# Cross-attention in a decoder: exponentials from key-by-token scores, heads from turned probabilities as stationary

## The chip, the cores and the metric

The kernel runs on one core of one Trainium2 chip. The metric is the device time of one launch in microseconds (us). The engines are TensorE (PE; its weight loads are PEld), VectorE (DVE), ScalarE (ACT), GpSimd (POOL) and SyncE (SP), which issues the DMAs. TensorE's clock is granted at 2.4 GHz (1.0 in the profile) or at half of it, 1.2 GHz (0.5).

## The reference

A decoder of four layers, each with self-attention, cross-attention and a feed-forward part, twelve sublayers, with `x = layernorm(x + sublayer(x))` after each. There are 32 sequences of 128 tokens and 128 features, all float32, and a context of 77 keys for each sequence. The change touches the cross-attentions of the layers 1, 2 and 3, which are of this kind (16 heads of 8 features):

```python
q = split_heads(xq @ Wq + bq); k = split_heads(xk @ Wk + bk); v = split_heads(xv @ Wv + bv)
logits = jnp.einsum('bhqd,bhkd->bhqk', q, k) / jnp.sqrt(8)
logits = logits + mask[None, None, :, :] * -1e9      # layer 2; layer 1 has no mask
weights = jax.nn.softmax(logits, axis=-1)
attn = jnp.einsum('bhqk,bhkd->bqhd', weights, v).reshape(B, S, 128)
return attn @ Wo + bo
```

Layer 3 has no biases, multiplies the scores by the square root of 8 and sets those where its mask (one row per sequence and token) is 0 to the lowest float32.

## The kernel before

A hardware loop makes four passes over eight sequences each. In a pass the twelve sublayers follow each other; their names in the code are L0A, L0X, L0F, L1A, L1X, L1F, L2A, L2X, L2F, L3A, L3X, L3F (A self-attention, X cross-attention, F feed-forward). The eight sequences are two groups `g` of four (`b`), a sequence is `j = 4 g + b`. Every engine runs its own program written out by hand, in order; semaphores (`wait_ge`, `then_inc`) tie them together. The weights of even layers share the buffer `w_even`, those of odd ones `w_odd`; SyncE loads a layer's weights once the layer two before is done. The rest lies in two arenas. PSUM has eight banks of 512 float32 columns.

The three cross-attentions L1X, L2X and L3X are built by one set of functions, `pe_context`, `act_context`, `dve_context` and `pool_context`; L3A, the self-attention of layer 3, uses some of the same helpers with 128 keys and keeps them in the change. Ahead of a stage `pe_context_part` and `act_context_part` make the keys and values of all eight sequences from the context: the keys in four copies (`C("res4")`), each with every fourth head's rows and zeros in the others, the values with zeros between (zeroed by GpSimd). So 32 rows of queries against one copy give four heads' scores with a contraction over 32 rows.

The unit of the loop is half a sequence, `u` of 16, which is 8 heads. In iteration `i` TensorE's program does

- `scores(i)` (L1402): two matmuls, 32 rows each, in the row groups 2 half + 0 and 1, tokens on the partitions, 4 x 77 columns each, into two of the four banks 0 to 3
- `pe_heads(i - 3)` (L1239): eight matmuls with 32 columns of values stationary and the turned probabilities moving
- `pe_probs_turn(i - 2)` (L1222): eight transposes of a head's 128x77 probabilities into banks 4 and 5.

Between them VectorE takes the maximum over the keys and subtracts it (L1290, L1292; with a mask, scale and mask first, L1283, then L1286 and L1288), ScalarE takes the exponential of 128x616 in SBUF (L1254), VectorE sums it and takes the reciprocal (L1299, L1301), GpSimd multiplies (L1314), and ScalarE and VectorE each copy one bank of turned probabilities out of PSUM (L1261, L1308). ScalarE adds the value bias to the heads of a group (L1267), and `pe_project_heads` (L1247) multiplies by Wo. The state is turned by `pe_turn_state` (L159) and multiplied by Wq (L1377). The second group's queries are made inside the loop, the first group's projection at `i == 12`; in L1X the first gate-up products of the next sublayer (L1539) lie between the last units.

A float32 matmul is two instructions in the profile, a transpose one.

## Time and profile before

| | |
|---|---|
| median of 3 runs | 5787.46 us |
| lowest and highest | 5780.36 and 5790.4 us |
| span of the profiled execution | 5793.5 us |
| instructions | 57753 |
| mean granted clock of TensorE | 0.836 |
| TensorE, VectorE, ScalarE, GpSimd busy | 85%, 51%, 33%, 18% |
| L1X, L2X, L3X in the first pass, first to last matmul | 107.7, 109.6, 110.5 us |

The profiled execution is one execution; its own time is the span, and it isn't among the three timed runs. Busy time is an average over twelve sublayers with different limits. The rows further down are the ones that bear on the three cross-attentions. Idle time stands in square brackets with what ended it. Where a line of the timeline has several instructions, the second number is the time from the first one's start to the last one's end, and the end of a matmul overlaps the start of the next.

### The profile page before, as it was taken

To read this page: it belongs to the slowest core of one execution; us is meant where nothing else is said; L and a number is where in the kernel's file an instruction comes from. 1 tells how busy PE (TensorE), PEld (TensorE's weight loads), DVE (VectorE), ACT (ScalarE), POOL (GpSimd) and SP (SyncE) were. 2 spreads that over 40 slices of the span, in tenths; PEclk is the share of its full clock that TensorE was granted. 3 is DMA by queue.
4 is the path that set the end of the run, shared out by engine and by line. 5 is a ranking of instruction groups with operands and counts; after the bars stand their busy time and mean duration, and the time that the engine had idled before them with its cause. 6 is when DMAs were issued, how large, how long until landed. Compare 5 with 4: busy or idle time off the path is not lost. (4 is left out here: it accounts for less than half of the span.)

```text
span 5793.5 us, 57753 instructions
## 1 busy us (share of the span) xinstructions
PE 4923.2 (85%) x20360; PEld 2783.9 (48%) x20360; DVE 2980.6 (51%) x6224; ACT 1939.1 (33%) x3508; POOL 1042.2 (18%) x876
## 2 busy tenths in 40 slices
PE   6888899989688889998968888998886888899888
PEld 4445454653444545465344454445534455545553
DVE  5555443763555544376355554446535555534643
ACT  4242222336324222233632422222364242223235
POOL 2021100213202110021320211002222021100222
PEclk8896879969799777996879987898597998789869
DMA  2000100000100010000010001000001000100000
GB/s 75 1 3 24 52 5 2 1 16 0 51 1 3 24 52 5 2 1 15 0 51 1 3 24 52 5 2 16 1 1 50 1 3 24 52 5 2 16 1 4
DMA packets 20876, 93.08 MB, mean 16 GB/s; under 512 B 5228, under 2 KB 14444, under 8 KB 17796
## 3 DMA queue, kind: packets, MB, share of 16 engines
q1 hardware_dynamic: 20580, 89.26, 4.1%
q8 instruction: 170, 2.79, 0.2%
q14 instruction: 126, 1.03, 0.1%
HBM read 87.16 MB, written 2.10 MB: 15 GB/s over the span
## 5 line engine op out<-in xcount | busy, mean ns | idle before, releaser
L1314 POOL TENSOR_TENSOR arena<-arena 128x616 f32<-128x616 f32 (+1 forms) x256 | 355.0, 1387 | 1189.2 <-DVE arena L1301 1188.8
L1254 ACT ACTIVATE arena<-arena 128x616 f32<-128x616 f32 (+1 forms) x256 | 205.2, 802 | 930.7 <-DVE arena L1288 481.2
L1222 PE MATMUL ps<-const,arena 128*77 128x128 f32 (+1 forms) x2048 | 422.0, 373 | 69.1 <-POOL arena L1314 69.1
L210 POOL TENSOR_SCALAR rstd_e<-mean_var 128x4 f32<-128x4 f32 x120 | 27.4, 228 | 2467.8 <-DVE mean_var L176 2467.8
L1923 DVE TENSOR_TENSOR arena<-ps,arena 128x512 f32<-128x512 f32 x256 | 176.5, 691 | 468.7 <-ACT arena L1873 468.7
L1222 PEld LDWEIGHTS ps<-const,arena 128*77 128x77 f32 (+1 forms) x2048 | 340.1, 207 | 153.6 <-POOL arena L1314 82.2
L1239 PE MATMUL ps<-arena,w_even 77*32 77x128 f32 (+1 forms) x2560 | 352.9, 355 | 50.8 <-DVE arena L1308 50.4
L1873 ACT ACTIVATE arena<-ps 128x512 f32<-128x512 f32 x288 | 172.0, 597 | 607.9 <-PE ps L1821 607.9
L1239 PEld LDWEIGHTS ps<-arena,w_even 77*32 77x32 f32 (+1 forms) x2560 | 264.3, 141 | 190.8 <-ACT arena L1261 87.1
L2263 PE MATMUL ps<-w_even,w_odd 128*128 128x512 f32 x640 | 321.6, 649 | 26.9 <-issue 26.9
L1308 DVE COPY arena<-ps 77x512 f32<-77x512 f32 (+1 forms) x256 | 174.5, 682 | 270.2 <-PE ps L1222 270.1
L1820 PE MATMUL ps<-xT,w_even 128*128 128x512 f32 x576 | 308.9, 618 | 3.1 <-DVE arena L1910 3.1
L1827 PE MATMUL ps<-arena,w_even 128*128 128x512 f32 x576 | 295.0, 594 | 7.0 <-DVE arena L1923 4.7
L745 PE MATMUL ps<-xT,w_even 128*128 128x512 f32 (+1 forms) x544 | 269.2, 618 | 0.4
L1821 PE MATMUL ps<-arena,w_even 128*128 128x512 f32 x512 | 266.3, 602 | 0.0
L1261 ACT ACTIVATE arena<-ps 77x512 f32<-77x512 f32 (+1 forms) x256 | 151.0, 590 | 328.7 <-PE ps L1222 328.5
L1402 PE MATMUL ps<-arena 32*128 32x308 f32 x768 | 211.3, 663 | 41.8 <-DVE arena L1288 25.2
L199 DVE TENSOR_TENSOR y_tok<-ps,x_tok 128x512 f32<-128x512 f32 x72 | 49.4, 686 | 357.3 <-PE ps L683 265.5
L1299 DVE TENSOR_REDUCE arena<-arena 128x8 f32<-128x616 f32 (+1 forms) x256 | 228.2, 892 | 0.5
L1559 PE MATMUL ps<-arena,w_odd 128*128 128x512 f32 x512 | 220.4, 592 | 0.0
L2263 PEld LDWEIGHTS ps<-w_even,w_odd 128*128 128x128 f32 x640 | 125.2, 205 | 186.9 <-issue 179.2
L2467 DVE SCALAR_TENSOR_TENSOR arena<-ps,arena 128x512 f32<-128x512 f32 x48 | 33.2, 692 | 343.8 <-ACT arena L2352 342.9
(383 smaller groups left out, 9365.4 us busy)
## 6 DMA issues: line engine op xcount, KB each, us to landing
w_even<-in_w SPq DMA_DIRECT2D x4, 6916.0 KB, 19.2
w_even<-in_w SPq DMA_DIRECT2D x4, 3313.5 KB, 10.9
w_odd<-in_w SPq DMA_DIRECT2D x4, 2824.5 KB, 9.4
w_odd<-in_w SPq DMA_DIRECT2D x4, 2095.0 KB, 8.2
w_odd<-in_w SPq DMA_DIRECT2D x4, 2048.0 KB, 15.2
x_in<-in_x SPq DMA_DIRECT2D x10, 256.0 KB, 2.8
w_odd<-in_w SPq DMA_DIRECT2D x4, 577.0 KB, 3.6
w<-in_w SPq DMA_DIRECT2D x1, 2050.0 KB, 10.7
```

Of the source, the lines that this page charges most:

```text
L745: mm = nc.tensor.matmul(ps[0:rows, k + i % 2, :], lhsT, xT[g][:, :], start=True, stop=True)
L1222: mm = nc.tensor.transpose(ps[0:nk, 4 + h // 4, (h % 4) * P:(h % 4 + 1) * P], m["P"][u % 3][:, h, :], ident)
L1239: mm = nc.tensor.matmul(ps[c0:c0 + 32, 6 + g, b * P:(b + 1) * P], m["v"][g][0:nk, b, r, c0:c0 + 32], m["PT"][0:nk, 4 * i + r, :], start=(r ...
L1254: nc.scalar.activation(p, p, ACT.Exp, scale=scale).then_inc(c_exp.sem, 1)
L1299: nc.vector.tensor_reduce(m["sum"][u % 3], m["P"][u % 3], AX.X, ALU.add)
L1314: nc.gpsimd.tensor_tensor(m["P"][u % 3], m["P"][u % 3], bcast(m["sum"][u % 3], m["nk"]), ALU.mult)\
L1402: mm = nc.tensor.matmul(ps[:, 2 * (u % 2) + i, 0:4 * KC], m["q"][g][r:r + 32, b * P:(b + 1) * P], m["k"][g][r:r + 32, b, :, :], start=True ...
L1559: mm = nc.tensor.matmul(bank(4 + n % 2), W(L1F, w)[:, k * T + c * P:k * T + (c + 1) * P], src[g][:, k, :], start=(k == 0), stop=(k == 3))
L1820: nc.tensor.matmul(bank(i % 2), w1, xT[g][:, :], start=True, stop=True)
L1821: nc.tensor.matmul(bank(2 + i % 2), w3, x3, start=True, stop=True).then_inc(e_gu.sem, 1)
L1827: nc.tensor.matmul(bank(6 + g), w, e_h[i % 2], start=(n == 0), stop=(n == 35)).then_inc(e_down.sem, 1)
L2263: nc.tensor.matmul(o, W(L3F, "ew2")[:, p * 384 + m * P:p * 384 + (m + 1) * P], i_hm[g][4 * (j - 1) + p], start=(p == 0), stop=False)
```

## The change

The scores are computed twice, once with the tokens on the partitions for the maximum alone, and once with the keys on the partitions for the exponential. A unit is a whole sequence, `j` of 8.

- `scores(j, p)`: the same two matmuls as before, for two values of `p`, now always into banks 0 and 1. `maxima` takes the negated maximum of them straight from PSUM. In L3X the mask is added in PSUM, by a bf16 matmul of the identity with the mask; in L2X VectorE adds it.
- `split_max` writes the 16 maxima as three bf16 parts, `turn_max` turns them with one bf16 transpose, and `by_head` spreads them (multiplied by the constant 0/1 columns `mrow`) into `less`, a moving operand of 512 columns.
- `turned_scores(j)`: four float32 matmuls, keys as stationary (32 rows x 77 columns) and queries in four copies as moving (512 columns), one in each row group, into banks 2 to 5. L2X first puts the mask into these banks with 16 transposes, L3X adds it with four bf16 matmuls. `less_max` adds the negated maximum with four bf16 matmuls.
- ScalarE reads these banks with the exponential and writes the turned probabilities to SBUF (four of 77x512 for a sequence). VectorE's subtraction, sums and copies, ScalarE's copies, GpSimd's multiplication and the 16 transposes of a sequence go.
- `heads(j)`: 16 matmuls with a head's turned probabilities (77x128) as stationary and its values with a column of ones (77x9) moving. `scaled` divides by the ninth column on VectorE, `turn_heads` turns the result, ScalarE copies it with the value bias.
- The queries are copied four times by ScalarE (`act_context_queries`), the keys once more. The end of the stage has another order. `w_loaded` uses two semaphores in place of ten.

```diff
+        def act_context_queries(act, L, g):
+            m = CB[L]
+            act.wait_ge(c_qc.sem, c_qc[L, g])
+            for r in range(4):
+                kw = {} if L == L3X else {"bias": m["bq"][:, r:r + 1]}
+                i = nc.scalar.activation(m["qx"][g][:, :, r, :], bank(6 + g).rearrange("p (b t) -> p b t", b=NB),
+                                         ACT.Identity, scale=m["rs"][:, r:r + 1], **kw)
+            i.then_inc(k_qx.sem, 1)
...
+                def scores(j, p):
...
+                    if j or p:
+                        pe.wait_ge(k_mr.sem, k_mr[L, j, p] - 1)
                     for i in range(2):
-                        r = 32 * (2 * half + i)
-                        mm = nc.tensor.matmul(ps[:, 2 * (u % 2) + i, 0:4 * KC], m["q"][g][r:r + 32, b * P:(b + 1) * P],
-                                              m["k"][g][r:r + 32, b, :, :], start=True, stop=True,
-                                              tile_position=(r, 0))
-                    mm.then_inc(c_sc.sem, 1)
+                        r = 32 * (2 * p + i)
+                        mm = nc.tensor.matmul(ps[:, i, 0:4 * KC], m["q"][g][r:r + 32, b * P:(b + 1) * P],
+                                              m["kx"][g][r:r + 32, b, :, :], start=True, stop=(L != L3X),
+                                              tile_position=(r, 0), skip_group_check=True)
+                    if L == L3X:
+                        for i in range(2):
+                            mm = nc.tensor.matmul(ps[:, i, 0:4 * KC], ident_bf[:, :], m["neg"][:, j, :]
+                                                  .rearrange("p (r k) -> p r k", r=1).to_broadcast([P, 4, KC]),
+                                                  start=False, stop=True, skip_group_check=True)
+                    mm.then_inc(k_s.sem, 1)
+
+                def turned_scores(j):
...
+                    for c in range(4):
+                        if j:
+                            pe.wait_ge(k_ex.sem, k_ex[L, j - 1, c])
+                        o = bank(2 + c)[0:KC, :]
+                        if L == L2X:
+                            for r in range(4):
+                                nc.tensor.matmul(o[:, r * P:(r + 1) * P], m["neg"], ident, is_transpose=True,
+                                                 start=(r == 0), stop=False, skip_group_check=True)
+                    for c in range(4):
+                        r = 32 * c
+                        nc.tensor.matmul(bank(2 + c)[0:KC, :], m["k"][g][r:r + 32, b * KC:(b + 1) * KC],
+                                         m["qx"][g][r:r + 32, b, :, :], start=(L != L2X), stop=False,
+                                         tile_position=(r, 0), skip_group_check=True)
+                    if L == L3X:
+                        for c in range(4):
+                            nc.tensor.matmul(bank(2 + c)[0:KC, :], ident_bf[0:KC, 0:KC],
+                                             m["negT"][:, j * P:(j + 1) * P].rearrange("p (r t) -> p r t", r=1)
+                                             .to_broadcast([KC, 4, P]), start=False, stop=False, skip_group_check=True)
+
+                def less_max(j):
+                    pe.wait_ge(k_mx.sem, k_mx[L, j])
+                    for c in range(4):
+                        r = 32 * c
+                        nc.tensor.matmul(bank(2 + c)[0:KC, :], ones_bf[r:r + 32, 0:KC], m["less"][j % 2][r:r + 32, :],
+                                         start=False, stop=True, tile_position=(r, 0), skip_group_check=True)\
+                            .then_inc(k_st.sem, 1)
...
+                def heads(j):
+                    if j:
+                        pe.wait_ge(k_oc.sem, k_oc[L, j - 1])
+                    for h in range(16):
+                        c, r = divmod(h, 4)
+                        if r == 0:
+                            pe.wait_ge(k_ex.sem, k_ex[L, j, c])
+                        mm = nc.tensor.matmul(heads_psum(j)[:, h, :], m["PT"][j % 2][:, c, r * P:(r + 1) * P],
+                                              m["v"][:, j, h, :], start=True, stop=True)
+                    mm.then_inc(k_pv.sem, 1)
...
+                for i in range(8 + 3):
+                    if i < 8:
+                        scores(i, 0)
                     if 0 <= i - 3:
-                        pe_heads(pe, L, i - 3)
-                    if 0 <= i - 2 < 16:
-                        pe_probs_turn(pe, L, i - 2)
-                    if i == 12:
+                        turn_heads(i - 3)
+                    if 0 <= i - 1 < 8:
+                        turn_max(i - 1)
+                        turned_scores(i - 1)
+                    if i == 1:
+                        pe_turn_state(pe, PREV[L], 1)
+                    if i < 8:
+                        scores(i, 1)
+                    if i == 2:
+                        pe.wait_ge(xT_ready.sem, xT_ready[PREV[L], 1])
+                        nc.tensor.matmul(bank(7), W(L, "Wq"), xT[1][:, :], start=True, stop=True)\
+                            .then_inc(c_qp.sem, 1)
+                    if 0 <= i - 1 < 8:
+                        less_max(i - 1)
+                    if 0 <= i - 2 < 8:
+                        heads(i - 2)
+                    if i == 7:
                         pe_project_heads(pe, L, 0)
```

ScalarE's loop is, for `i` from 1 to 10, `heads(i - 3)` (the copy), the state's copy at 1, `act_context_queries` at 2, `exps(i - 1)`. VectorE's is `maxima(i, 0)`, `by_head(i - 1)`, `maxima(i, 1)`, `split_max(i)`, the norm of the state at 0, the second group's queries at 2, `scaled(i - 2)`, and the first group's sum at 8 and norm at 9. GpSimd does the bias sums and the norms' powers alone.

## Rows read from the trace of the kernel before

**Rows 1.** The page: busy time, share of the span, instructions.
```profile
PE 4923.2 (85%) x20360; PEld 2783.9 (48%) x20360; DVE 2980.6 (51%) x6224; ACT 1939.1 (33%) x3508; POOL 1042.2 (18%) x876
```

**Rows 2.** Windows: L1X in three passes, L2X twice, L3X, middle of L1X.
```profile
core 0: us, PE busy (x) PEld busy (x) DVE busy (x) ACT busy (x) POOL busy (x), PEclk, DMA share, GB/s
449.81:557.50 107.69, 93.86 (x482) 65.23 (x482) 57.78 (x109) 24.47 (x38) 24.46 (x22) 0.62 0.07 28
1903.82:2003.49 99.67, 85.58 (x482) 59.78 (x482) 57.76 (x109) 24.46 (x38) 24.46 (x22) 0.67 0.08 30
3354.45:3444.22 89.77, 74.44 (x482) 52.97 (x482) 57.29 (x109) 24.35 (x38) 24.47 (x22) 0.77 0.09 33
...
675.62:785.18 109.56, 92.95 (x482) 66.43 (x482) 70.44 (x148) 23.21 (x37) 23.24 (x21) 0.58 0.12 50
...
1158.38:1268.85 110.47, 93.43 (x470) 65.38 (x470) 70.20 (x139) 22.51 (x36) 22.00 (x20) 0.58 0.06 20
461.00:523.00 62.00, 61.31 (x283) 41.36 (x283) 32.54 (x51) 14.28 (x22) 13.35 (x12) 0.50 0.00 1
```

**Rows 3.** Timeline of TensorE in L1X (start, us, group): low clock, then full.
```profile
482.42 1.40 PE L1402 MATMUL ps<-arena 32*128 32x308 f32 x4
483.74 2.78 PE L1239 MATMUL ps<-arena,w_even 77*32 77x128 f32 x16
486.45 1.99 PE L1222 MATMUL ps<-const,arena 128*77 128x128 f32 x8
488.37 1.40 PE L1402 MATMUL ps<-arena 32*128 32x308 f32 x4
...
528.32 1.10 PE L1222 MATMUL ps<-const,arena 128*77 128x128 f32 x8
529.35 0.79 PE L1402 MATMUL ps<-arena 32*128 32x308 f32 x4
```

**Rows 4.** Timeline: matmuls that move 8 columns, at low and at full clock.
```profile
1277.41 3.58 PE L2294 MATMUL ps<-w_odd,arena 32*128 32x8 f32 x16
...
817.92 1.06 PE L1786 MATMUL ps<-w_even,xT 128*128 128x8 f32 x8 [0.69 <-ACT xT L167]
```

**Rows 5.** Timeline of TensorE in L3A: one matmul of 32 rows, both clocks.
```profile
1059.61 2.07 PE L1999 MATMUL ps<-w_even 32*128 32x512 f32 x2
...
1072.11 1.12 PE L1999 MATMUL ps<-w_even 32*128 32x512 f32 x2
```

**Rows 6.** Timeline of TensorE in L3F: two bf16 matmuls at low clock.
```profile
1312.28 1.09 PE L2241 MATMUL ps<-arena,expand 8*128 8x512 bf16 x2 [0.26 <-ACT arena L2327]
```

**Rows 7.** Groups by line and form, L1X, first pass: busy us, mean ns.
```profile
L1290 DVE TENSOR_REDUCE arena<-ps 128x8 f32<-128x616 f32 x16 | 12.6, 790 | 11.6 <-PE ps L1402 11.6
L1261 ACT ACTIVATE arena<-ps 77x512 f32<-77x512 f32 x16 | 9.5, 593 | 33.1 <-PE ps L1222 33.1
L1267 ACT ACTIVATE arena<-ps,w_even 128x512 f32<-128x512 f32 x2 | 1.4, 680 | 3.6 <-PE ps L1239 3.6
```

**Rows 8.** Timeline of VectorE in L3F: a split into three bf16 parts.
```profile
1285.62 0.18 DVE L669 CAST arena<-arena 128x32 bf16<-128x32 f32 x1
...
1286.66 0.18 DVE L677 CAST arena<-arena 128x32 bf16<-128x32 f32 x1
```

**Rows 9.** One line's instructions: duration in ns, least, median, most.
```profile
L1343 ACT ACTIVATE arena<-ps,arena,const x64: 600/626/654, 437.8 to 4990.6; 128x308 f32<-128x308 f32 x64
```

**Rows 10.** Timeline of ScalarE ahead of L1X: the values' copies.
```profile
448.00 0.78 ACT L300 ACTIVATE w_even<-ps 77x128 f32<-77x128 f32 x4 [1.11 <-PE ps L1330]
```

**Rows 11.** Timeline of TensorE at the end of L1X, around a rise.
```profile
544.63 1.99 PE L1222 MATMUL ps<-const,arena 128*77 128x128 f32 x8
546.42 0.90 PE L159 MATMUL ps<-const,x_tok 128*128 128x128 f32 x4
```

**Rows 12.** Windows after a rise and before a fall, columns as in rows 2.
```profile
714.30:721.00 6.70, 5.58 (x50) 4.10 (x50) 6.22 (x12) 1.79 (x3) 2.58 (x3) 1.00 0.01 2
...
533.40:536.60 3.20, 0.22 (x3) 0.04 (x2) 3.13 (x9) 1.20 (x2) 0.99 (x2) 1.00 0.00 0
```

More of the change, by code:

```diff
@@ L1088, in act_l1a @@
             result(1)
+            act_context_queries(act, L1X, 0)
             act_context_part(act, L1X, "v")
@@ L1147, in build @@
         SMALL = [L1X, L2X, L3A, L3X]
+        CROSS = [L1X, L2X, L3X]
         U = range(16)
-        us = [(L, u) for L in SMALL for u in U]
+        us = [(L3A, u) for u in U]
         lg = [(L, g) for L in SMALL for g in G]
@@ new lines, in self_buffers @@
+            e = Carve(0, w_even, cols[L3X]["_width"])
+            o = Carve(0)
+            m["S"] = [e.take(NB * 16 * P).rearrange("p (m t) -> p m t", t=P),
+                      a.take(NB * 16 * P).rearrange("p (m t) -> p m t", t=P)]
+            m["v"] = [t.take(NB * 4 * P).rearrange("p (b r d) -> p b r d", b=NB, r=4) for t in (e, a)]
+            m["k"] = [t.take(NB * 4 * P).rearrange("p (b r k) -> p b r k", b=NB, r=4) for t in (e, w)]
+            m["q2"] = e.take(NG * T)
+            m["q"] = m["oT"] = [m["q2"][:, g * T:(g + 1) * T] for g in G]
@@ L1201, in buffers @@
+            m["Q"] = [o.take(16 * P).rearrange("p (t b h) -> p t b h", b=NG * NB, h=16) for _ in range(2)]
+            m["bk"] = a.take(4)
+            m["rs"] = a.take(4)
+            o = Carve(0, start=4352)
+            m["P"] = [o.take(8 * P).rearrange("p (m k) -> p m k", m=8) for _ in range(3)]
             m["PT"] = a.take(8 * P).rearrange("p (m q) -> p m q", m=8)
@@ L1351, in dve_context_columns @@
+        SCALE = {L1X: 1.0, L2X: float(np.float32(8.0) ** np.float32(-0.5)),
+                 L3X: float(np.float32(8.0) ** np.float32(0.5))}
         def dve_context_columns(dve, L):
             m = CB[L]
-            dve.wait_ge(w_loaded[L].sem, 16)
+            dve.wait_ge(*w_loaded(L))
+            nc.vector.tensor_scalar(m["rs"], C("res4"), SCALE[L], None, ALU.mult)
             if L != L3X:
                 nc.vector.tensor_scalar(m["bk"], C("res4"), W(L, "bk"), None, ALU.mult)
+                nc.vector.drain()
+                nc.vector.tensor_scalar(m["bq"], m["rs"], W(L, "bq"), None, ALU.mult)
@@ L1426, in run @@
                 if L == L1X:
+                    pe_turn_state(pe, L1X, 0)
+                    pe_l1f_gate_up(pe, 0)
                     pe_l1f_gate_up(pe, 1)
+                if L == L2X:
+                    pe_l2f_route(pe, 0)
                 pe_project_heads(pe, L, 1)
@@ L1456, in run @@
                 if L == L2X:
+                    act_copy_state(act, L2X, 0, xT[0][:, :])
                     act_l2f_exps(act, 0)
@@ L1483, in run @@
+                    if 0 <= i - 2:
+                        scaled(i - 2)
+                    if i == 8:
+                        dve_sum(dve, L, 0)
+                    if i == 8 and L == L1X:
+                        dve_l1f_scales(dve)
+                    if i == 9:
+                        dve_normalise(dve, L, 0, x_tok[0])
                 if L == L2X:
```

338 lines of the change are left out of this document (213 added, 125 removed).

## The prediction

> **What bounds the kernel now.** I read the page first. TensorE is busy 85% of the span, VectorE 51%, ScalarE 33%, GpSimd 18% [rows 1], but these are averages over twelve layers, and the change touches three stages. So next the stretches from the first to the last matmul of each. L1X takes 107.7, 99.7 and 89.8 us in the first three passes, the fourth like the third (mean 96.7), L2X 109.6 in the first and 113.1 in the others (mean 112.3), L3X 110.5 in all four [rows 2]. L1X is the same work every time; what differs is the granted clock, 0.62 to 0.77. In its middle (461 to 523 us) TensorE is busy 61.3 of 62 us at a clock of 0.50, while VectorE has 32.5 us to do. Hence the timeline of TensorE, where a half sequence (8 heads) is three steps: scores 1.32 us (482.42 to 483.74), heads 2.71, eight transposes 1.92, together 5.95, then the next begins. At full clock the transposes take 1.03, and the pair of score matmuls 0.79 in its own row [rows 3]. TensorE sets these stages wherever its clock is 1.2 GHz. So what GpSimd, VectorE and ScalarE are relieved of counts little; what counts is what TensorE is given to do for a sequence, against 11.9 us now, and at which clock.
>
> **The change, on TensorE, per sequence (16 heads), at 1.2 GHz.**
>
> Removed: 16 transposes (3.84) and the old heads (5.42). The four key-by-key score matmuls (two pairs, 2.64) stay, for the maximum alone.
>
> Heads with the probabilities as stationary: 16 float32 matmuls that move nine columns. They are bound by loading 128 columns: the row nearest in kind is L2294, 32x128 stationary and 8 moving columns, 16 instructions in 3.58 us, 0.22 each; the 128-row L1786 at full clock has 1.06 for eight, of which I count 0.92 (the next line begins then), 0.115 each [rows 4]. A float32 matmul is two instructions in these rows, so 32 x 0.22 = 7.0 us (3.7 at 2.4 GHz). 32 and 128 rows cost alike, so 77 will. This is more than the old heads.
>
> Turned scores: four matmuls of 32 rows x 512 columns, one in each row group. One alone is 2.07 at 1.2 GHz and 1.12 at 2.4 in its row, some 2.0 and 1.05 from its start to the next line's [rows 5]. Two in two row groups overlap: each moving 308 columns, they take 1.32, and 308/512 of 2.0 is 1.2. I take full overlap of four, 2.0; above, overlap only in pairs, 4.0. The Trainium skill, "TensorE: Matmul & The Clock Gate", section "Part 3: Packing small matmuls — row/col tiling", gives 3.07 for four row tiles of 512 columns instead of 4. By it the step is 8.0/3.07 = 2.6 us, and the sum would be 0.6 x 96 = 58 us more.
>
> The split maximum taken off: four bf16 matmuls of 512 columns, also by row group. Two in sequence take 1.09 [rows 6], about 0.5 each; overlapped 0.5, in pairs 1.0, in sequence 2.0. I take 0.5. Two single transposes (maximum in bf16, heads) at 0.15 to 0.25: 0.4.
>
> Sum for L1X: 2.6 + 2.0 + 0.5 + 7.0 + 0.4 = 12.5, against 11.9. L2X adds 16 transposes that put the mask into the turned scores, 16 x 0.24 = 3.8: 16.3. L3X adds four bf16 matmuls of 512 columns and four of 308: 1.8 + 1.1 = 2.9: 15.4. At 2.4 GHz the three are 6.7, 8.8 and 8.3.
>
> **The other engines.** VectorE: four reductions of 308 columns (616 take 0.79) 1.6, five small casts and subtractions (1285.62 to 1286.84) 1.2, one multiplication of 512 columns from PSUM 0.7 at the same rate, reciprocal and scaling at most as much: 4.2 us; L2X adds four additions of 308, near 6 [rows 7, 8]. ScalarE: four exponentials of 77x512 at 0.6 and a small copy, 2.7. GpSimd has nothing left but bias and norm. All are below TensorE, even at 2.4 GHz. Within an iteration the 3.7 to 7 us of heads stand between the maximum's matmuls and the next turned scores, which hides the exponentials; the turned scores hide the maxima, whose banks 0 and 1 are now single. So I cost these waits at nothing; without that cover ScalarE's 2.4 us would stand open.
>
> **Around the loop.** Before the values ScalarE now issues four copies of the queries (4 x 0.68) and two more of the keys (2 x 0.63); the values take two copies of 0.6 for twice 0.78 [rows 7, 9, 10]; queued behind them are the values for which the first scores wait: 2.2 us later in L1X and L3X (I let the keys' part overlap), 0.3 in L2X. The rest of L1X: queries 2.1, two turns of the state 1.9, two projections 3.1, the first two gate-up products 6.3 and some 6 us of waits at both ends: 19.4. At the end x_tok is normalised only after the last heads are scaled, so turn, copy and gate-up, which lay between units before, stand in a row. L2X: 14. L3X: 9. The old stages have 14 to 17 us in which TensorE is not busy [rows 2]; I have not carried them over but counted the new ends step by step. The weight transfers wait for the same stage ends as before; one semaphore for several layers costs nothing.
>
> All at 1.2 GHz: L1X 8 x 12.5 + 19.4 = 119.4; L2X 8 x 16.3 + 14 = 144.4; L3X 8 x 15.4 + 9 = 132.2.
>
> **The clock.** It is the largest unknown. In L1X it stayed at 1.2 GHz for ten units with no idle time. It rose near 547, right after eight transposes and amid four more, all of full height, and after another rise it was 1.00 for 6.7 us. It fell at the end of 3.2 us in which TensorE was busy 0.22 [rows 11, 12]. The nine-column matmuls stayed at 1.2 when they began there [rows 4]. For L1X and L3X I therefore take 1.2 GHz, with one short rise at the projection of the first four sequences: 2 us back in L1X; in L3X, where mask matmuls of full height stand beside the turned scores, 5 us. In L2X every sequence has 3.8 us of full-height transposes and 2.0 of turned scores: I let the clock rise in each, and fall in the heads. A stretch of 5 to 6 us at 2.4, somewhat less than that 6.7, does the work of 10 to 12: 5 us back a sequence, 40 in the stage.
>
> L1X 119.4 + 2.2 - 2 = 119.6 against 96.7: +22.9. L2X 144.4 + 0.3 - 40 = 104.7 against 112.3: -7.6. L3X 132.2 + 2.2 - 5 = 129.4 against 110.5: +18.9. Sum +34.2 a pass, times 4: +137 us. The profiled execution gives 5793.5 + 137 = 5930; its span is 0.1% above the median of the timed runs (5787.5), so I forecast 5787.5 + 137 = 5924.
>
> **Rivals.** *Transposes do not lift the clock.* Then L2X stays at 1.2 GHz, +32 instead of -8, and the sum is (23 + 32 + 19) x 4 = +297: 6085. Against it, the rise among transposes [rows 11]; for it, the long low stretch that is one third transposes [rows 3]. The Trainium skill, same page, section "Part 4: PE-mode transpose", says that they do not count as busy for the clock. By that rule this rival is the forecast; the trace speaks against it [rows 11, 12].
>
> *The clock is up for most of the three stages (the other side).* Four row groups work at once in the turned scores, more of the array than any old step of these stages used, and L1X itself ran at 0.77 in two passes [rows 2]. With 5 us back in every sequence of every stage: L1X 81.6 (-15), L2X 105 (-8), L3X 94 (-16), times 4: -156, 5632. It decides from 34 us more a pass than I give, about 2 us more for each sequence of L1X and L3X. At 2.4 GHz throughout, the stages would be some 70, 88 and 82 us: -320, 5470. Against it: more than half of a sequence's time is heads that stream nine columns.
>
> *The row groups overlap only in pairs.* 2.0 + 0.5 us more for each of 96 sequences: +240 on top, 6160. For it: no row shows four at once.
>
> *No effect.* GpSimd's and VectorE's waits at the stages' ends go away and the clock gives a little more, so that gain and loss cancel: 5787.
>
> **How the numbers follow.** Forecast with L1X and L3X low and L2X lifted in part: 0.52, its own range 5840 to 6000, from 3 to 7 us back in L2X and from none to 2 back in L3X. Transposes that don't lift: 0.14. Clock mostly up: 0.20. Pairs: 0.08. Cancelled: 0.06. A change within 0.2%, 12 us, is about what a measurement of this kernel can't tell from none. Slower 0.52 + 0.14 + 0.08 = 0.74, same 0.06, faster 0.20. The range 5760 to 6090 takes in the forecast, the cancelled case, the first rival and the edge of the second, and leaves out the deeper gains and the pairs.
>
> **What would show it.** Nine-column matmuls at 0.22 us an instruction (0.115 at full clock), 32 a sequence: if they are near 0.11 at 1.2 GHz, the largest term is wrong. Four turned-score matmuls starting within some ns of each other and over in 2.0 us. In L1X a period of 12.5 us a sequence at clock 0.50 with TensorE without idle time; in L2X one of about 11 with the clock between 0.6 and 0.8, up in the turned scores and down in the heads. ScalarE's and VectorE's releases must not end TensorE's waits inside the loop. A clock over 0.7 in L1X or L3X would make the forecast wrong, so would a TensorE that waits for exponentials or maxima.

## The result, and the profile after

The changed kernel takes 5838.3 us (median of 6 runs, 5827.2 to 5843.6), the kernel before took 5788.6 us beside it (6 runs, 5777.2 to 5794.3). The ratio is 1.0067, with a 95% interval from 1.0036 to 1.0097: slower, by about 50 us. The forecast was 5924 us, 137 us slower: the direction was right, the size was nearly three times too large. The profiled execution has a span of 5825.5 us, 32 us above that of before: it is the shortest of the six, 11 us under their median, and the profiled one of before is 5 us above its own. Every table by stage here comes from one profiled execution of a kernel.

First the page, its row for busy time, then windows of the stages (first matmul of the scores to last of the projection): L1X in the first two passes, L2X in the first two, L3X in the first and the third. The answers before are [rows 1, 2].

```profile
PE 5044.5 (87%) x20968; PEld 2864.4 (49%) x20968; DVE 2680.8 (46%) x6309; ACT 1972.4 (34%) x3632; POOL 781.9 (13%) x708
```

```profile
core 0: us, PE busy (x) PEld busy (x) DVE busy (x) ACT busy (x) POOL busy (x), PEclk, DMA share, GB/s
449.57:556.93 107.36, 101.60 (x466) 69.55 (x466) 35.81 (x120) 24.50 (x48) 5.05 (x6) 0.57 0.06 25
1902.91:2007.28 104.37, 98.45 (x466) 66.72 (x466) 36.09 (x122) 24.50 (x48) 5.04 (x6) 0.59 0.06 26
...
671.82:772.03 100.21, 91.90 (x594) 72.94 (x594) 50.11 (x155) 26.03 (x51) 3.81 (x5) 0.77 0.15 63
2120.78:2225.58 104.80, 96.26 (x594) 75.90 (x594) 50.10 (x155) 26.04 (x51) 3.81 (x5) 0.73 0.14 60
...
1148.26:1266.47 118.21, 112.09 (x518) 71.17 (x518) 35.14 (x114) 22.36 (x47) 2.51 (x4) 0.60 0.04 16
...
4056.37:4168.82 112.45, 106.33 (x518) 67.30 (x518) 35.14 (x114) 22.36 (x47) 2.51 (x4) 0.64 0.04 18
```

VectorE's and GpSimd's work is down (in L1X 57.8 to 36.1 us, 24.5 to 5.0), TensorE's is up, and TensorE is busy 92 to 95% of these stages. The three stages in a table (us, sums over four passes; "between" is everything else of the span):

| | before | after | difference | forecast |
|---|---|---|---|---|
| L1X | 386.9 | 418.8 | +31.9 | +91.6 |
| L2X | 449.0 | 414.6 | -34.4 | -30.4 |
| L3X | 441.9 | 467.1 | +25.2 | +75.6 |
| between | 4515.7 | 4525.0 | +9.3 | 0 |

So L2X came out as forecast, and two thirds of what L1X and L3X were to lose did not appear. Now the timeline of TensorE: a sequence of L1X with the clock at 0.50 and later heads of the same stage, one of L2X, one of L3X (start in us, us of the group, lines; instructions are x).

```profile
476.33 7.00 PE L1522 MATMUL ps<-w_even,arena 77*128 77x9 f32 x32
483.26 1.40 PE L1466 MATMUL ps<-arena 32*128 32x308 f32 x4
484.59 0.47 PE L1528 MATMUL ps<-const,arena 128*128 128x128 f32 x1
484.85 0.31 PE L1513 MATMUL ps<-ident_bf,arena 128*128 128x128 bf16 x1
485.10 2.00 PE L1490 MATMUL ps<-w_even,arena 32*77 32x512 f32 x8
486.88 0.64 PE L1503 MATMUL ps<-arena,ones_bf 32*77 32x512 bf16 x2
486.89 1.24 PE L1466 MATMUL ps<-arena 32*128 32x308 f32 x4
487.92 0.64 PE L1503 MATMUL ps<-arena,ones_bf 32*77 32x512 bf16 x2
488.49 7.00 PE L1522 MATMUL ps<-w_even,arena 77*128 77x9 f32 x32
...
500.61 3.99 PE L1522 MATMUL ps<-w_even,arena 77*128 77x9 f32 x32
...
719.55 3.32 PE L1486 MATMUL ps<-const,arena 128*77 128x128 f32 x16
722.80 1.10 PE L1490 MATMUL ps<-w_odd,arena 32*77 32x512 f32 x8
...
724.56 3.74 PE L1522 MATMUL ps<-arena 77*128 77x9 f32 x32
...
1174.04 2.00 PE L1490 MATMUL ps<-w_even,arena 32*77 32x512 f32 x8 [1.14 <-ACT arena L1580]
1175.98 1.93 PE L1495 MATMUL ps<-w_even,ident_bf 77*77 77x512 bf16 x4
...
1180.37 7.00 PE L1522 MATMUL ps<-w_even,arena 77*128 77x9 f32 x32
```

L1522 are the heads, L1466 the scores, L1490 the turned scores, L1486 and L1495 the mask, L1503 the maximum taken off. In L1X the period is 488.49 - 476.33 = 12.16 us, without an idle gap; 12.5 was forecast. The nine-column instructions take 7.00 / 32 = 0.22 us. Four turned-score matmuls are over in 2.00 us. The second pair of scores (486.89) runs in the row groups that the maximum's matmuls leave free. In L3X the next heads begin at 1195.90, 15.53 us after 1180.37 (forecast 15.4). The waits inside the loop, which the forecast put at nothing, are small: in the first pass 2.2 us for the split maxima in L2X's first two sequences and 1.1 us for exponentials in L3X (the row at 1174.04). The costs at the lower level of the clock were right; what was not is how long the clock stayed there.

### The profile page after: what moved, and what is told of

It reads as the page before. It is cut to its first block and busy times, and to the rows that moved or that the text cites. A ratio compares the mean times of both kernels' runs of the same rounds, so it can differ in the third digit from the quotient of the medians.

```text
span 5825.5 us, 58910 instructions
## 1 busy us (share of the span) xinstructions
PE 5044.5 (87%) x20968; PEld 2864.4 (49%) x20968; DVE 2680.8 (46%) x6309; ACT 1972.4 (34%) x3632; POOL 781.9 (13%) x708
## 5 line engine op out<-in xcount | busy, mean ns | idle before, releaser
L1522 PEld LDWEIGHTS ps<-w_even,arena 77*128 77x128 f32 x2048 | 367.1, 281 | 34.5 <-issue 27.0
L1522 PE MATMUL ps<-w_even,arena 77*128 77x9 f32 x2048 | 373.1, 325 | 3.3 <-ACT arena L1589 3.3
L1580 ACT ACTIVATE arena<-ps 77x512 f32<-77x512 f32 x384 | 196.1, 591 | 184.4 <-PE ps L1503 184.4
L1466 PE MATMUL ps<-arena 32*128 32x308 f32 x768 | 206.2, 624 | 47.0 <-DVE arena L1632 20.5
L823 ACT ACTIVATE arena<-ps,w_even 128x512 f32<-128x512 f32 (+1 forms) x136 | 93.4, 687 | 332.3 <-PE ps L752 332.3
L1632 DVE TENSOR_REDUCE arena<-ps 128x4 f32<-128x308 f32 x256 | 110.5, 473 | 206.2 <-PE ps L1471 137.8
L1666 DVE RECIPROCAL arena<-ps 128x16 f32<-128x16 f32 x96 | 24.7, 257 | 378.5 <-PE ps L1522 378.5
L2033 PEld LDWEIGHTS ps<-arena,w_even 128*128 128x128 f32 x576 | 108.8, 190 | 148.3 <-issue 133.8
L1330 POOL TENSOR_TENSOR arena<-arena 128x1024 f32<-128x1024 f32 x64 | 121.3, 1896 | 407.7 <-DVE arena L1317 407.3
L2740 POOL TENSOR_TENSOR w_even<-w_even,arena 128x512 f32<-128x512 f32 x128 | 143.9, 1151 | 221.7 <-ACT arena L2534 130.0
```

The source lines that it names most:

```text
L1466: mm = nc.tensor.matmul(ps[:, i, 0:4 * KC], m["q"][g][r:r + 32, b * P:(b + 1) * P], m["kx"][g][r:r + 32, b, :, :], start=True, stop=(L != ...
L1522: mm = nc.tensor.matmul(heads_psum(j)[:, h, :], m["PT"][j % 2][:, c, r * P:(r + 1) * P], m["v"][:, j, h, :], start=True, stop=True)
L1580: nc.scalar.activation(m["PT"][j % 2][:, c, :], bank(2 + c)[0:KC, :], ACT.Exp, scale=scale)\
L2033: nc.tensor.matmul(bank(6 + g), w, e_h[i % 2], start=(n == 0), stop=(n == 35)).then_inc(e_down.sem, 1)
L2740: nc.gpsimd.tensor_tensor(i_hm[g][4 * k + p], i_h[g][p], i_mb[g][4 * k + p], ALU.mult)\
```

## The experiments

All are built from the changed kernel unless they say otherwise. The ratio in each is to the kernel before, run beside it; the changed kernel has 1.0067. The kernel before itself came out between 5752 and 5837 us in these comparisons, with medians from 5777.7 to 5799.8, so the ratio counts more than the time. Three dots in an edit stand for lines left out.

**Mask transposes of L2X left out.**

```diff
-                        if L == L2X:
-                            for r in range(4):
-                                nc.tensor.matmul(o[:, r * P:(r + 1) * P], m["neg"], ident, is_transpose=True,
-                                                 start=(r == 0), stop=False, skip_group_check=True)
...
-                nc.vector.tensor_scalar(m["neg"], W(L, "mask"), -1000000000.0, None, ALU.mult)
+                nc.vector.tensor_scalar(m["neg"], W(L, "mask"), 0.0, None, ALU.mult)
```

> The changed kernel without the 16 transposes that put L2X's mask into its turned scores (the mask of L2X is left out altogether, its column of negated values is zero; all other work stays). Theory: full-height transposes raise the clock for the turned scores and heads behind them and so pay for themselves. Without them a sequence of L2X is one of L1X: the stage comes to L1X's 104.4 us less its own extras, 104.4 - 19.4 + 14 = 99 us, against 104.8 with them: -6 us a pass, 5815 us in all, and the granted clock of L2X falls from 0.73 to about 0.6. Rival: the transposes are a plain cost and the clock rises as often without them: the 3 us that they take in each sequence go, -24 us a pass, 5740 us.

Measured: 5837.0 us, 1.0071 (1.0049 to 1.0094), as with them. Window of L2X in the second pass:

```profile
2124.94:2231.34 106.40, 98.75 (x466) 68.93 (x466) 50.13 (x155) 26.07 (x51) 3.81 (x5) 0.55 0.14 59
```

128 instructions fewer (466 for 594), and the stage takes 106.4 us instead of 104.8: the clock is 0.55 in place of 0.73. Over the four passes L2X takes 425.5 us without them and 414.6 with them. The 16 transposes of a sequence cost nothing, because the clock rises after them. "Transposes do not lift the clock" falls.

**The same transposes, of zeros, added to L1X.** The result stays the reference's.

```diff
-                        if L == L2X:
+                        if L in (L1X, L2X):     # m["neg"] is zero in L1X
...
-                                         m["qx"][g][r:r + 32, b, :, :], start=(L != L2X), stop=False,
+                                         m["qx"][g][r:r + 32, b, :, :], start=(L == L3X), stop=False,
```

> The changed kernel with 16 float32 transposes of zeros added to each sequence of L1X, into the banks of the turned scores, where L2X has its mask transposes; the result is the same. Theory: they lift the clock, and L1X takes L2X's period of 10.0 us a sequence in place of 12.15 in those that are at 1.2 GHz and 9.15 in those that rose: 8 x 10.0 + 19.4 = 99 against 104.4: -5 us a pass, 5818 us, clock of L1X from 0.59 to 0.7 or more. Rival: they are only added work, 16 x 0.24 us at 1.2 GHz or 16 x 0.12 at 2.4: +15 to +31 us a pass, 5900 to 5960 us.

Measured: 5831.5 us, 1.0057 (1.0037 to 1.0077). L1X in the second pass:

```profile
1896.73:2001.37 104.64, 97.87 (x594) 75.24 (x594) 36.08 (x122) 24.50 (x48) 5.04 (x6) 0.76 0.06 25
```

104.6 us for 104.4 with 128 instructions more, and the clock at 0.76 for 0.59. The 5 us of gain expected are not there, the 15 to 31 us of the rival neither: work that lifts the clock paid for itself once more (417.8 us over four passes, for 418.8).

**Short full-height matmuls among the heads of L1X and L3X.**

```diff
                                               m["v"][:, j, h, :], start=True, stop=True)
+                        if L != L2X:
+                            for _ in range(2):
+                                mm = nc.tensor.matmul(ps[:, 6 + j // NB, 384:512], ident_bf[:, :], ident_bf[:, :],
+                                                      start=True, stop=True, skip_group_check=True)
```

> The changed kernel with two bf16 matmuls of the identity by itself (128 rows, 128 columns, into a free part of the heads' bank, never read) after each of the 16 heads in L1X and L3X. Theory: what keeps these stages at 1.2 GHz is that the nine-column matmuls of the heads keep little of the array at work; with full-height work among them the clock stays at 2.4 GHz, where heads take 3.7 and the added 32 matmuls at most 32 x 0.055 = 1.8 us. A sequence of L1X is then 6.7 + 1.8 = 8.5 us against 12.15, of L3X 10.1 against 15.5; L1X about 83 us (-20 or so), L3X about 95 (-23): -170 us in all, 5660 us. Rival: the clock of these stages does not depend on it; then the added matmuls cost 32 x 0.11 = 3.5 us a sequence at 1.2 GHz, +28 us a stage, +224 us: 6060 us.

Measured: 5961.1 us, 1.0284 (1.0244 to 1.0325). L1X and L3X in the second pass:

```profile
1942.51:2058.66 116.15, 110.28 (x722) 79.11 (x722) 36.08 (x122) 24.54 (x48) 5.05 (x6) 0.62 0.06 23
2655.53:2787.80 132.27, 127.29 (x774) 83.94 (x774) 35.16 (x114) 22.39 (x47) 2.52 (x4) 0.61 0.04 15
```

The clock stayed near where it was (0.62 and 0.61; in L1X 0.58 in two of the passes), and the 256 added instructions cost 15 us a pass in L1X and 16 in L3X (477.4 - 418.8 and 531.2 - 467.1, by four), a little over half of the rival's 28. My expectation was wrong: full-height work in this amount and form, spread through the heads, does not hold the clock, while a block of 16 transposes raises it. The two differ in type (bf16 and float32), in kind (matmul and transpose) and in place (spread and in one block); which of these matters is not shown, since no block of plain matmuls was tried.

**The change in L2X alone, and in L1X and L3X alone.** Both programs hold the old functions and the new ones, and a list says which stage has which.

```diff
-        CROSS = [L1X, L2X, L3X]
+        CROSS = [L2X]               # the other kernel: [L1X, L3X]
```

> The change made in L2X alone; L1X and L3X are built as before. Theory: the stages are independent and the whole is the sum of stage effects: L2X gains 449.0 - 414.6 = 34.4 us a launch, L1X and L3X go back to their old 386.9 and 441.9 us: 5787 - 34 = about 5755 us, 0.5 to 0.7% faster than before. Rival: what is gained in L2X is given back at its ends (the stretch behind L2X grew by 3.5 us a pass): no more than 0.3% faster, 5770 us or more.

> The change made in L1X and L3X alone; L2X as before. Theory A: stage effects add up and each stage has its own time whatever is around it: L1X 418.8 and L3X 467.1 us as in the changed kernel, L2X back at 449.0: 5838 + 34 = 5872 us. Theory B, after the L2X-only kernel, in which the unchanged L1X ran in 338 us at a clock of 0.83 in place of 387 at 0.71: the clock that a stage gets depends on when it starts, and the same stage comes out differently when the work around it shifts; then L1X is 5 us or more a pass away from 104.7, or L2X from 112.3, in either direction.

Measured: new L2X alone 5711.3 us, 0.9856 (0.9816 to 0.9895). New L1X and L3X with the old L2X: 5817.0 us, 1.0063 (1.0030 to 1.0095). Windows of the first: L1X (old) in the first two passes; then of the second: L2X (old) in the first two.

```profile
447.92:530.79 82.87, 67.55 (x482) 48.61 (x482) 57.41 (x109) 24.35 (x38) 24.48 (x22) 0.86 0.09 36
1874.64:1959.81 85.17, 70.23 (x482) 50.57 (x482) 57.37 (x109) 24.35 (x38) 24.48 (x22) 0.82 0.09 35
```

```profile
675.00:771.84 96.84, 74.74 (x482) 55.16 (x482) 69.28 (x148) 22.42 (x37) 23.22 (x21) 0.74 0.13 57
2120.70:2229.35 108.65, 96.55 (x482) 67.41 (x482) 70.75 (x148) 23.42 (x37) 23.21 (x21) 0.56 0.12 51
```

Of the first kernel's 82 us (span 5711.8), L2X gave 449.0 - 419.4 = 30 us, as expected. But 48 us came from the L1X that nobody had touched: 338.4 us instead of 386.9, with the same 482 matmul instructions and the clock at 0.82 to 0.86 instead of 0.62 to 0.77 [rows 2]. In the other kernel the old L2X took 96.8 us in two passes and 108.7 and 109.9 in the others, against 113.1 in three passes of before. Stage effects do not simply add up: an old stage gets another clock when the work around it changes. Of theory B the size came true in L2X (9 us a pass away from 112.3), not in L1X (1.7 us away from 104.7); its reason, the moment of the start, is not shown.

What sets the old L1X's times apart is when the clock rises. Windows of the kernel before, first pass, then third pass ahead of the rise and after it; then of new L2X alone, first pass, ahead of the rise and after it.

```profile
455.00:526.00 71.00, 66.29 (x304) 45.81 (x306) 38.12 (x61) 16.31 (x25) 15.82 (x13) 0.50 0.04 16
...
3360.00:3386.50 26.50, 22.14 (x96) 14.95 (x97) 14.11 (x23) 5.96 (x9) 6.08 (x5) 0.50 0.09 38
3387.00:3421.00 34.00, 30.87 (x265) 23.06 (x264) 30.65 (x58) 12.58 (x20) 12.22 (x11) 1.00 0.01 1
```

```profile
452.00:472.00 20.00, 15.06 (x70) 10.63 (x68) 13.08 (x23) 4.72 (x8) 5.24 (x5) 0.50 0.19 80
472.50:512.50 40.00, 35.21 (x295) 25.91 (x296) 35.01 (x65) 13.48 (x22) 14.19 (x13) 1.00 0.00 1
```

In the kernel before the rise inside the loop comes 77, 56 and 32 us after the stage's first matmul in the first three passes, with new L2X alone after 24 us, and from then on the clock stays up until TensorE waits 3 us for VectorE near the end of the loop. The earlier the rise, the shorter the stage: 107.7, 99.7, 89.8 and 82.9 us. What decides the moment is open.

**The same L1X begun a little later**, in the kernel before.

```diff
+                    if u == 0 and L == L1X:
+                        for _ in range(4):
+                            nc.tensor.matmul(ps[:, 2, 384:393], ident, ident[:, 0:9], start=True, stop=True)
```

> The kernel before with four more float32 matmuls of nine columns (never read) ahead of L1X's first scores, 0.9 us at 2.4 GHz or 1.8 at 1.2, in each pass, nothing else. Theory: the same L1X gets another clock when it starts at another moment; the added work is 4 to 7 us in all, but L1X comes out 5 us or more a pass away from its 107.7, 99.7, 89.8 and 89.8 us, up or down, so that the total is off by more than what was added. Rival: the differences between passes and kernels come from something else (data, the neighbouring stages), and all of L1X, L2X and L3X stay as they were but for the added 1 to 2 us: 5793 us.

Measured: 5783.2 us (12 runs, 5752.8 to 5842.3), 0.9996 (0.9963 to 1.0030). Inconclusive: the median did not move, and the runs of both kernels spread over 76 to 90 us (before: 5752.5 to 5828.8). The profiled execution took 5842.3 us, the longest of the twelve, so its stages are not compared. That the moment of the start decides is not shown.

**All turned-score matmuls of L1X in one row group**, those for the maximum too; three quarters of L1X's scores are computed from other heads' rows.

```diff
-                        r = 32 * c
+                        r = 0 if L == L1X else 32 * c      # in turned_scores and less_max
```

> The changed kernel with the four turned-score matmuls and the four that take off the maximum of L1X all in row group 0 instead of one in each (same shapes and count; the other groups' heads are left out of L1X's scores, so the result of L1X is another). Theory: the four groups run at once; in one group the turned scores take 4 x 2.0 = 8.0 us in place of 2.0 and the maximum's 4 x 0.5 = 2.0 in place of 0.5, part of it beside the scores of groups 2 and 3: +6 to +7.5 us a sequence, +48 to +60 us a pass if the clock stays, and the clock of L1X falls from 0.59 to 0.50, since fewer rows work at once, for another 5 to 10 us: +53 to +70 a pass, 6050 to 6120 us. Rival: the groups hardly overlap and the 2.0 us of the profile is something else (queued issue): less than +15 us a pass, below 5900 us.

Measured: 6051.4 us, 1.0452 (1.0377 to 1.0526). L1X in the second pass, the inside of its loop in the first pass, and a piece of its timeline:

```profile
1951.49:2110.98 159.49, 153.50 (x466) 89.91 (x466) 36.17 (x122) 24.44 (x48) 5.04 (x6) 0.52 0.04 17
...
450.00:600.00 150.00, 146.36 (x441) 86.79 (x440) 30.91 (x101) 23.41 (x47) 2.54 (x3) 0.50 0.00 1
```

```profile
1988.20 4.55 PE L1490 MATMUL ps<-w_even,arena 32*77 32x512 f32 x5
1991.69 1.40 PE L1466 MATMUL ps<-arena 32*128 32x308 f32 x4
1992.54 2.76 PE L1490 MATMUL ps<-w_even,arena 32*77 32x512 f32 x3
1995.10 1.91 PE L1503 MATMUL ps<-arena,ones_bf 32*77 32x512 bf16 x4
```

159.5 us instead of 104.4, +55 a pass, inside the expected 53 to 70. The eight instructions take from 1988.20 to 1995.10, 6.9 us instead of 1.8 (485.10 to 486.88): the four row groups do work at once, 3.9 times as fast as one. "Only in pairs" falls. The clock, too, shows something: in none of the four passes does it rise inside L1X's loop (0.50 from 450 to 600 us), where in the changed kernel it rises three or four times a pass. So what lifts the clock there in the changed kernel is the work of the row groups together; the turned scores and the maximum's matmuls were moved at once, so which of the two counts is not separated.

**ScalarE's copies of the first queries behind the values.**

```diff
-            act_context_queries(act, L1X, 0)
             act_context_part(act, L1X, "v")
+            act_context_queries(act, L1X, 0)       # and the same for L3X
```

> The changed kernel with ScalarE's four copies of the first group's queries issued behind the copies of the values in L1X and L3X, not ahead of them. Forecast's step: the copies ahead of the values make the first scores of L1X and L3X 2.2 us late. Theory after the trace of the changed kernel: only 1.5 us of it is there, in L3X alone, so L3X starts 1.5 us earlier a pass, L1X not, and the turned scores, which need these copies, take back part: 0 to -1.5 us a pass, 5832 to 5838 us, no difference that can be measured. Rival: the first term was right, only hidden by something else: -4 us a pass, 5820 us.

Measured: 5837.2 us, 1.0090 (1.0060 to 1.0120), no difference from the changed kernel. The stretches ahead of L1X and L3X got 2.0 and 5.4 us shorter over four passes, L1X and L3X 3.5 and 2.6 us longer: the copies can stand before or behind, the turned scores need them either way.

**Heads by column group in L1X and L3X.** The values are stationary again, and four matmuls in a row go to four different column groups; a second set with ones gives the sums.

```diff
+    for o, st in ((0, m["v"][g][0:KC, b]), (16 * 9, None)):
+        for r in range(4):
+            for c in range(4):
+                w = m["one"][0:KC, r, :] if st is None else st[:, r, 32 * c:32 * c + 32]
+                mm = nc.tensor.matmul(ps[32 * c:32 * c + 32, 6 + g, o:o + P], w,
+                                      m["PT"][j % 2][:, c, r * P:(r + 1) * P],
+                                      start=(r == 0), stop=(r == 3), tile_position=(0, 32 * c),
+                                      skip_group_check=True)
+    # VectorE, scaled(j):
+    nc.vector.reciprocal(m["inv"], turned_psum(j))
...
+    nc.vector.tensor_tensor(m["on"][j % 2], ps[:, 6 + j // NB, 0:P], m["inv"], ALU.mult)
```

> The changed kernel with other heads in L1X and L3X, with the same result: the values stationary again (77x32, three quarters zeros, as before the change), turned probabilities moving, 16 matmuls that go round the four column groups instead of staying in one, and 16 more with ones in place of the values for the sums; VectorE divides one 128x128 block by the other, and no transpose of the heads is left. Theory: TensorE sets these stages, and the nine-column heads are their largest term (7.0 us at 1.2 GHz) because each loads 128 columns to stream nine. 64 instructions of 128 columns took 0.17 us each in one column group; if four column groups overlap as the four row groups did, 64 x 0.17 / 4 = 2.7 us, a sequence of L1X 8.0 us at 1.2 GHz and L3X 11.2, and with more of the array at work the clock rises more often: L1X 104 to about 80, L3X 118 to about 100, -40 us a pass, 5680 us. Rival: column groups do not overlap: heads and sums take 64 x 0.17 = 10.9 us, +3.9 us a sequence, +60 us a pass, 6080 us. Second rival: VectorE or ScalarE sets the stages; then the time stays within 20 us of the changed kernel.

Measured: 5615.3 us, 0.9693 (0.9624 to 0.9762). Timeline: the heads with their sums at 1.2 and at 2.4 GHz; windows: L1X and L3X in the first pass.

```profile
487.02 3.64 PE L1541 MATMUL ps<-arena,w_even 77*32 77x128 f32 x64
...
503.17 1.96 PE L1541 MATMUL ps<-arena,w_even 77*32 77x128 f32 x64
```

```profile
451.87:532.54 80.67, 70.21 (x714) 38.43 (x714) 41.14 (x120) 24.81 (x48) 5.04 (x6) 0.64 0.08 33
1126.99:1212.10 85.11, 74.46 (x766) 36.42 (x766) 40.43 (x114) 22.54 (x47) 2.29 (x3) 0.75 0.06 22
```

64 instructions take 3.64 us at 1.2 GHz where 32 nine-column ones took 7.00. At one column group's 0.17 us each [rows 3] they would have taken 10.9, so the groups overlap, 3.0 times instead of 4. L1X fell to 80.7 us in the first pass, as expected; L3X fell by 27 to 33 us a pass, more than expected, with its clock at 0.75 in place of 0.60. VectorE's work in L1X went up from 36 to 41 us while the stage got shorter: TensorE sets these stages, and the nine-column heads were their largest term.

**The same in L2X.** The edit adds L2X to the list; half of its values go to free columns of the other arena, and its mask buffers move to the weights' buffer.

```diff
+                vs = (Carve(0, start=7168), a) if L == L2X else (w, w)
```

> The kernel with heads by column group in L1X and L3X (5615 us), and now in L2X too, same result. In the former the 64 matmul instructions of heads and sums took 3.64 us at 1.2 GHz and 1.96 at 2.4, against 7.0 and 3.74 for the nine-column ones. Theory: TensorE sets L2X too. Its period was 9.97 us with heads of 3.74 at 2.4 GHz and transposes mostly at 1.2; heads of 1.96 at 2.4 GHz leave 8.2, at the most one of VectorE's waits (near 6 us of work a sequence): 8 x 8.2 + 16 = 82 to 86 against 102: -17 us a pass, 5615 - 68 = 5547 us, 4.2% faster than before. Rival: in L2X VectorE, with the additions of the mask and now a 128x128 reciprocal and division, becomes the bound: 95 us or more a stage, 5590 us or more.

Measured: 5571.8 us, 0.9634 (0.9607 to 0.9661). L2X takes 91.3 us, between the two expectations. Its timeline shows a new wait, ahead of the transpose of the maxima:

```profile
695.10 0.22 PE L1529 MATMUL ps<-ident_bf,arena 128*128 128x128 bf16 x1 [1.69 <-DVE arena L1701]
695.15 2.87 PE L1502 MATMUL ps<-const,w_odd 128*77 128x128 f32 x16
```

L1701 is VectorE's division, the last thing in its sequence. What stands behind the wait on TensorE, the 16 mask transposes, needs nothing from it.

**The transpose of the maxima issued later.**

```diff
+                    if L == L2X or j == 0 or j == NB:     # in turned_scores, behind the mask transposes
+                        turn_max(j)
...
+                    if not (L == L2X or j == 0 or j == NB):     # behind the turned scores
+                        turn_max(j)
...
                     if 0 <= i - 1 < 8:
-                        turn_max(i - 1)
                         turned_scores(i - 1)
```

> The kernel with heads by column group in all three stages (5572 us), with the transpose of the maxima issued later on TensorE: in L2X behind the 16 mask transposes, in L1X and L3X behind the turned scores (but ahead of them in the first sequence of each group). Same work, same result. Theory: with shorter heads TensorE now waits inside the loop for VectorE (1.69 us before this transpose in L2X, 0.8 in L1X when the clock is up); the moved work covers that wait: -1.5 us a sequence in L2X, up to -0.8 in L1X and L3X, -10 - 4 - 4 us a pass, about 5500 us. Rival: the wait only moves on to the matmuls that take off the maximum, which now have 1.1 to 2.0 us less from the transpose to them for VectorE's 0.7 us of spreading; then less than 20 us of it is left, 5550 us or more.

Measured: 5504.5 us, 0.9500 (0.9485 to 0.9515). Windows of L1X, L2X and L3X in the second pass, and L2X's timeline:

```profile
1824.56:1904.64 80.08, 69.92 (x714) 37.14 (x714) 41.10 (x120) 24.81 (x48) 5.04 (x6) 0.66 0.08 33
2019.71:2098.53 78.82, 65.79 (x842) 45.80 (x842) 54.38 (x155) 26.35 (x51) 3.82 (x5) 0.86 0.19 80
2479.67:2559.23 79.56, 69.39 (x766) 34.45 (x766) 40.36 (x114) 22.65 (x47) 2.29 (x3) 0.78 0.06 23
```

```profile
688.15 1.97 PE L1502 MATMUL ps<-const,w_odd 128*77 128x128 f32 x16
689.96 0.22 PE L1533 MATMUL ps<-ident_bf,arena 128*128 128x128 bf16 x1
690.11 1.10 PE L1508 MATMUL ps<-w_odd,arena 32*77 32x512 f32 x8
691.04 0.69 PE L1482 MATMUL ps<-arena 32*128 32x308 f32 x4
692.17 0.41 PE L1523 MATMUL ps<-arena,ones_bf 32*77 32x512 bf16 x4 [0.44 <-DVE arena L1693]
```

A wait of 1.69 us has become one of 0.44, at the place that the rival named, and the clock stays up through most of L2X (0.86). Most of the gain is there (-12.5 us a pass), some in L3X (-5.7), none in L1X (+2.2); the stretches between grew by 4.7. The profiled executions are 45 us apart (5553.2 and 5507.8), the medians 67, since the profiled one of the kernel before this step was the shortest of its six. This kernel does what both others do, 5.0% faster than before the change.

## Why the forecast was right in sign and wrong in size

**Which engine sets the end: right.** TensorE's share of the stages went up, VectorE lost 38% of its work in L1X (57.8 to 36.1 us) and half in L3X (70.2 to 35.1), GpSimd 80 to 90%, and the time did not fall with it. Other heads on TensorE in two of the stages took 3.7% off (5615 against 5838 us); what ScalarE's other order gained ahead of the stages came back within them.

**Costs of a sequence at 1.2 GHz: right.** 12.16 us for 12.5 in L1X and 15.53 for 15.4 in L3X; heads 7.0, turned scores 2.0, the maximum 0.5 hidden in part beside the second scores. The row groups overlap: one group alone costs 55 us a pass, 6.9 us in place of 1.8 for the turned scores of a sequence, 3.9 times. The Trainium skill's 3.07 for four row tiles ("TensorE: Matmul & The Clock Gate", "Part 3: Packing small matmuls — row/col tiling") would have given 2.6 us; here it was 2.00.

**The clock of L2X: right in amount, not in place.** 104.7 us forecast, 103.7 measured (mean of four). That transposes lift the clock was the step on which this hung; taking them out of L2X and putting them into L1X both showed it (0.73 to 0.55, 0.59 to 0.76). The Trainium skill says in "Part 4: PE-mode transpose" of the same page that a transpose does not count as busy for the clock; in these runs it does, and the measurement decides. But I had let the clock rise for the turned scores and fall in the heads. It was up in both, with heads of 3.74 us, and low for the most part in the transposes (3.32 us for 16).

**The clock of L1X and L3X: the step that failed.** "For L1X and L3X I therefore take 1.2 GHz, with one short rise at the projection ... 2 us back in L1X; in L3X ... 5 us." With the measured periods and my own terms around the loop, L1X at 1.2 GHz throughout would be 8 x 12.16 + 19.4 = 116.7 us and took 104.7 on average: 12 us back, not 2. (The rows of the first pass bear the 19.4 out: 13.7 us of work outside the eight periods and 5.8 us of waits.) L3X would be 8 x 15.53 + 9 = 133.2 and took 116.8: 16 back, not 5. (Its first pass shows 5.7 us of such work and 6.1 of waits, nearer 12 than 9, which would make it 19 back.) In the timeline the clock rises after the turned scores, the maximum's matmuls and the scores, and the heads that follow run at 2.4 GHz for the greater part (from 500.61 3.99 us, not 7.00), and then it falls. The reason that the forecast had for staying low, that more than half of a sequence is heads that stream nine columns, fits the fall but gives no reason against a rise; with the turned scores in one row group L1X's clock did not rise at all inside the loop. The rival with the clock mostly up named this mechanism and a size of 5 us a sequence; it came to 1.5 in L1X and 2 in L3X. Of a miss of 105 us against the spans (137 - 32), this step makes 4 x (10 + 11.4) = 86. The late start, which does not lie inside these stages, makes 17.6, the periods 6.7 and L2X 4, less 9 that the stretches between grew. Why some sequences rise and others of the same work don't is not shown.

**Around the loop.** The late start that I had put into the stages lies ahead of them: the stretches before L1X and L3X grew by 6.6 and 13.7 us over four passes, 20 us for my 17.6. That the sizes agree is in good part luck: with the queries' copies behind the values, the stretches gave back only 7.4 of these 20 us, and where the rest comes from is open. The one before L2X became 11.4 us shorter, at a clock of 0.94 and 0.95 instead of 0.93 in the first two passes; I had nothing for that.

**The base of the comparison.** I took the old stages' times as theirs. They are not fixed: the same old L1X took 82.9 to 107.7 us in the profiles of these kernels. So "+32 us in L1X" says as much about the clock that the old one happened to get as about the new one, and in the kernel with the new L2X alone it took 48 us less over the four passes. The changed kernel's 50 us are more than the medians of the kernel before differ by (22 us), but less than its single runs do (84 us).

**What the change itself does.** The new L2X took 409 to 420 us in the seven kernels that have it with its mask and nine-column heads, the old one 449 and, in one kernel, 412: a gain of 30 to 40 us beside before, none beside that one. In L1X and L3X it replaces 9.3 us of heads and transposes by 7.0 of nine-column heads, 2.0 of turned scores and the maximum's 0.5, and in L3X 2.9 of masks; TensorE gains nothing, and VectorE's relief has no taker. With heads sent round the column groups it pays (5615 us), but that the gain needs the change is not shown: the old heads go four times in a row to one column group (5.42 us a sequence), and the kernel before with its heads sent round the groups was not built. If their 32 instructions overlapped like the 64 in 3.64 us, they would take 1.8 us, and an old sequence 11.9 - 5.4 + 1.8 = 8.3 us at 1.2 GHz by this estimate, where the one with new heads by column group took 8.8 (487.02 to 495.82).

## What to carry to other kernels

Where TensorE sets the time, count its instructions by what each measured: one that streams nine columns against a 128-column stationary took 0.22 us here at 1.2 GHz, more than one that streams 128 columns against 32 (0.17), and small matmuls sent round the row or column groups in turn cost a quarter or a third. Price such a stage at both levels of the clock, with the row that shows what stood before a rise, and treat the clock of the old stage as a variable too: judge by several passes and builds before giving a stage credit for it. When a stage has been shortened, look for the next wait and for work behind it that does not need it; here moving one transpose was worth as much as L2X's new heads: 67 and 43 us by the medians, 45 and 67 by the profiled executions.

## What was not expected of the hardware

- Work that raised the clock was free: 16 transposes more or fewer in each of eight sequences changed a stage of the second pass by 0.3 us (L1X) and 1.6 us (L2X), with the granted clock at 0.76 for 0.59 and 0.73 for 0.55.
- Two bf16 matmuls of 128 columns after every nine-column pair did not raise it (0.62 and 0.61) and cost 15 and 16 us a stage.
- Four row groups: 1.8 us for what takes 6.9 in one, and with one alone the clock never rose inside the stage's loop. Four column groups: 3.64 us for 64 instructions, 10.9 by the rate of one group.
- The same instructions of a stage got a clock from 0.62 to 0.86 in the old L1X and from 0.55 to 0.74 in the old L2X, depending on the kernel and the pass. In the old L1X the clock, once up, stayed up until a wait of 3 us; in the new one it fell again within the nine-column heads.
